# Last mixture of a decoder kernel: the gathers are spread over the pairs of experts, the answer rows are added on VectorE before they are turned, and unread matmuls stand in every second pair

## The reference, cut to what matters

```python
# x: [1792, 128] tokens, normalised; E = 32 experts, top 2, capacity 70 each
scores = softmax(router(x, stats(x)))            # [1792, 32]
w, e = top2(scores); w = w / w.sum(-1)
for each expert i:
    rows = the 70 best-scored tokens of those that chose i   # fewer: some slots stay empty
    h = silu(x[rows] @ gate_i.T) * (x[rows] @ up_i.T)        # 2 blocks of 128, and a
    y = h @ down_i.T + 0.05 * adapter_of_pair(x[rows])       # third from the pair's adapter
    out[rows] += w[rows, i] * y
x = x + out
```

## Time and profile before

| | us |
|---|---|
| median of 3 runs | 3799.75 (3795.43 to 3820.61) |
| profiled execution, its own time | 3812.16 |
| its span, first to last instruction | 3810.4 |
| last mixture: first gather issued | 3684.58 |
| first up matmul | 3689.53 |
| end of the last up (pair 15) | 3784.10 |
| first answer chunk read back | 3796.70 |
| last add to `x` | 3806.61 to 3807.23 |
| mean granted TensorE clock over the span | 0.948 |

### The profile page before, as it was taken

The page is one execution under the profiler, slowest core; times in us unless marked ns, Lnnn a source line. Parts: engine busy times, 40 slices in busy tenths (PEclk is TensorE's granted clock), DMA queues, the critical chain, the costliest instruction groups (busy, mean ns, idle before and its releaser), DMA issues. The chain is left out here.

```text
span 3810.4 us, 110666 instructions
## 1 busy us (share of the span) xinstructions
PE 3447.9 (90%) x46768; PEld 2411.7 (63%) x46768; DVE 2381.6 (63%) x4435; ACT 2087.9 (55%) x3581; POOL 1618.1 (42%) x1884
## 2 busy tenths in 40 slices
PE   7986669999999697889999999799999999999878
PEld 5654237777777344657777777343446777777548
DVE  5523568877776354468877776233667877777552
ACT  4333557777777222147777776334446777776511
POOL 1100157677674000047777664000336776776121
PEclk9999979999999798899999999899999999999967
DMA  4054136665664243036666564110015666656423
GB/s 164 2 227 168 47 84 155 153 159 144 154 156 97 51 117 82 4 88 152 149 160 148 149 158 100 47 61 23 13 43 140 156 154 152 159 145 153 123 68 106
DMA packets 206109, 439.22 MB, mean 115 GB/s; under 512 B 88210, under 2 KB 101111, under 8 KB 205448
## 3 DMA queue, kind: packets, MB, share of 16 engines
q1 hardware_dynamic: 202760, 430.07, 42.7%
q0 software_dynamic: 1440, 1.83, 0.2%
q10 hardware_dynamic: 1440, 0.52, 0.1%
HBM read 184.67 MB, written 5.40 MB: 50 GB/s over the span
## 5 line engine op out<-in xcount | busy, mean ns | idle before, releaser
L1562 DVE TENSOR_REDUCE x_bank_top<-ps 112x1 f32<-112x500 f32 x2304 | 1414.2, 672 | 447.8 <-PE ps L1264 440.8
L1410 ACT ACTIVATE x_probs_t<-ps 128x896 f32<-128x896 f32 x768 | 703.3, 916 | 127.6 <-PE ps L1285 122.6
L1264 PE MATMUL ps<-x_keys,x_queries 96*112 96x500 bf16 x2304 | 653.6, 382 | 42.5 <-DMA x_queries<-x_query_part 18.6
L1285 PEld LDWEIGHTS ps<-x_queries,x_keys 128*128 128x128 bf16 x9216 | 509.2, 97 | 245.6 <-issue 139.8
L1285 PE MATMUL ps<-x_queries,x_keys 128*128 128x112 bf16 x9216 | 580.9, 213 | 5.4 <-ACT x_probs_t L1410 4.2
L1299 PE MATMUL ps<-x_probs_t,x_values 128*32 128x112 f32 x18432 | 483.4, 261 | 8.9 <-ACT x_probs_t L1412 8.9
L1299 PEld LDWEIGHTS ps<-x_probs_t,x_values 128*32 128x32 f32 x18432 | 436.9, 110 | 70.1 <-issue 39.4
L1488 POOL TENSOR_TENSOR x_key_part<-x_key_whole,x_nothing 128x500 bf16<-128x500 f32 x270 | 337.3, 1249 | 256.8 <-ACT x_key_whole L1394 256.8
L1412 ACT ACTIVATE x_probs_t<-ps 128x448 f32<-128x448 f32 x768 | 414.5, 540 | 0.0
L1264 PEld LDWEIGHTS ps<-x_keys,x_queries 96*112 96x112 bf16 x2304 | 262.6, 131 | 170.9 <-DVE x_bank_top L1562 69.8
L1496 POOL TENSOR_TENSOR x_key_part<-x_key_left,x_nothing 128x500 bf16<-128x500 f32 x270 | 335.8, 1244 | 14.1
(11 more groups left out here) (510 smaller groups left out, 4332.1 us busy)
## 6 DMA issues: line engine op xcount, KB each, us to landing
x_keys<-x_key_part SPq DMA_DIRECT2D x1152, 192.0 KB, 3.8
x_ctx_t<-in_ctx_t SPq DMA_DIRECT2D x96, 750.0 KB, 6.2
cm_ctx_n<-in_ctx_n SPq DMA_DIRECT2D x32, 768.0 KB, 6.2
cm_ctx_t<-in_ctx_t SPq DMA_DIRECT2D x32, 750.0 KB, 8.6
x_queries<-x_query_part SPq DMA_DIRECT2D x558, 28.0 KB, 2.5
e_share<-m_weight_rows SPq DMA_DIRECT2D x32, 448.0 KB, 6.0
m_w<-in_L_ffn_experts SPq DMA_DIRECT2D x16, 768.0 KB, 5.7
e_share<-m_weight_rows SPq DMA_DIRECT2D x8, 896.0 KB, 5.3
```

Of the source, the lines that this page charges most:

```text
L1264: nc.tensor.matmul(ps[0:RW, n, 0:KB], queries[i // 2 % 2][0:TALL, p, i % 2, :], keys[i % 2][0:TALL, p, KB * n:KB * n + KB], start=True, st ...
L1285: mm = nc.tensor.matmul(ps[:, turned_bank(i, p) + c // VC, RW * (c % VC):RW * (c % VC) + RW], keys[i % 2][:, p, KT * c:KT * c + KT], queri ...
L1410: nc.scalar.activation(goal[:, 0:VR - 1], ps[:, bank:bank + VR - 1, 0:VC * RW], ACT.Exp, scale=scale).then_inc(exp_done, 1)
L1562: nc.vector.tensor_reduce(bank_top[0:RW, p, n:n + 1], ps[0:RW, n, 0:KB], AX_X, ALU.max).then_inc(topped, 1)
```

## The change

- The groups of tiles become 0 and 1, 2 and 3, 4 to 7, 8 to 11, 12 to 15, 16 and 17 (`GROUPS`).
- POOL issues only the first 8 gathers in a row. The other ten follow one at a time, gather 8 + n once up(n) is done, each ahead of the scatters of pair n - 1.
- PE runs six unread matmuls instead of four ahead of the first transposes, one more ahead of up(0), one behind it, and one ahead of up(n + 1) for n = 0, 2, ..., 14, into bank `TURN` and after a wait for the copy of the groups that pair n + 1 needs.
- ACT loads the table for Silu ahead of the first copy of a group, rather than at the first Silu.
- At the end PE waits for the last `weigh` and runs ten unread matmuls. DVE adds the two answer halves in SBUF (`join`), and PE turns the sum with one transpose for each block instead of two matmuls. DVE's order is join(0), join(1), add(0), join(2), add(1), join(3), add(2), add(3).

```diff
-    FIRST, GROUP = 2, 4
+    GROUP, AHEAD = 4, 8
+    GROUPS = (0, 2, 4, 8, 12, 16, TILES)
...
         last = (2 * CAP * (min(n, PAIRS - 1) + 1) - 1) // P
-        return max(last - FIRST, -1) // GROUP + 2
+        return next(g for g in range(len(GROUPS)) if GROUPS[g] > last)
...
-        return range(max(FIRST + GROUP * (g - 1), 0), min(FIRST + GROUP * g, TILES))
+        return range(GROUPS[g], GROUPS[g + 1])
...
-            def stay_busy(n):
+            def stay_busy(n, bank=RESULT + 1):
                 for _ in range(n):
-                    nc.tensor.matmul(ps[:, RESULT + 1, 0:CT], chip.mean[:], chunk[0], start=True, stop=True)
+                    nc.tensor.matmul(ps[:, bank, 0:CT], chip.mean[:], chunk[0], start=True, stop=True)
...
-            stay_busy(4)
+            stay_busy(6)
...
             for g in range(groups_for(0)):
                 turn_gathered(g)
+            stay_busy(1)
             up(0)
+            stay_busy(1)
             for g in range(groups_for(0), groups_for(1)):
                 turn_gathered(g)
             for n in range(PAIRS + 1):
                 if n + 1 < PAIRS:
+                    if n % 2 == 0:
+                        pe.wait_ge(s["gathered_kept"], groups_for(n + 1))
+                        stay_busy(1, TURN)
                     up(n + 1)
...
-            for c in range(CH):
-                pe.wait_ge(answers_landed[c], 16)
+            pe.wait_ge(s["weighted"], TILES)
+            stay_busy(10)
+            for c in range(CH):
+                pe.wait_ge(s["joined"], c + 1)
                 for t in range(TC):
-                    for k in range(2):
-                        mm = nc.tensor.matmul(ps[:, c, PAIR * t:PAIR * t + PAIR], back[c][:, t, k, :], chip.ident[0:PAIR, 0:PAIR], start=(k == 0), stop=(k == 1))
+                    mm = nc.tensor.transpose(ps[:, c, PAIR * t:PAIR * t + PAIR], back[c][:, t, 0, :], chip.ident[0:PAIR, 0:PAIR])
                 mm.then_inc(s["summed"], 1)
...
+            nc.scalar.preload_act_table_set("silu_and_others")
             for g in range(groups_for(0)):
                 keep_gathered(g)
...
-            for j in range(TILES):
+            def gather(j):
                 nc.gpsimd.indirect_dma_start(gathered[:, j, :], None, table, ...).then_inc(gathered_landed[j], 16)
-            pool.wait_ge(s["emptied"], 16 * CH)
-            for j in range(TILES):
+            def scatter(j):
                 r = slice(0, lines_in(j))
                 pool.wait_ge(s["weighted"], j + 1)
...
+            for j in range(AHEAD):
+                gather(j)
+            pool.wait_ge(s["emptied"], 16 * CH)
+            for n in range(PAIRS + 1):
+                if AHEAD + n < TILES:
+                    pool.wait_ge(s["up_done"], n + 1)
+                    gather(AHEAD + n)
+                for j in finished(n - 1):
+                    scatter(j)
...
-            for c in range(CH):
+            def join(c):
+                dve.wait_ge(answers_landed[c], 16)
+                nc.vector.tensor_tensor(back[c][:, :, 0, :], back[c][:, :, 0, :], back[c][:, :, 1, :], ALU.add).then_inc(s["joined"], 1)
+
+            def add(c):
                 goal = x[:, CB * c:CB * c + CB, 0:S]
                 dve.wait_ge(s["summed"], c + 1)
                 nc.vector.tensor_tensor(goal, goal, ps[:, c, 0:CT].rearrange("p (b s) -> p b s", s=S), ALU.add).then_inc(s["added"], 1)
+
+            join(0)
+            for c in range(1, CH):
+                join(c)
+                add(c - 1)
+            add(CH - 1)
```

More of the change, by code:

```diff
@@ L1970, in mixture_3 @@
             " gathered_turned gathered_kept up_done gate_kept hidden_ready down_done down_kept result_turned weighted slot_chain slots_ready"
-            " scattered summed added stored")
+            " scattered joined summed added stored")
     s = {k: chip.sem("m3_" + k) for k in sems.split()}
```

## The result

The changed kernel takes 3780.48 us in the median of 20 runs (3764.4 to 3792.89), the kernel before 3798.39 us over 20 (3782.85 to 3826.18). The ratio is 0.9941, with a 95% interval of 0.9925 to 0.9957. The forecast was 3778, range 3760 to 3798. The profiled execution takes 3780.02 us, 32.1 less than the one before, where the sum said 32.0. Of these 32.1 us the part that the change touches gives 30.6 (28.5 in the pairs, 2.1 at the end); 1.6 come from the stages ahead of it, which nobody changed: the first gather is issued at 3682.97 instead of 3684.58. The medians are only 17.9 us apart.

What follows compares the result with a forecast made beforehand. PE was taken as the bound, at half clock for much of the changed last 126 us. Terms -26.9 - 5.5 + 5.3 - 1.5 + 0.2 - 3.6 = -32.0 us from 3812.16 gave 3780; forecast 3778 us, range 3760 to 3798.

Steps and rivals of the forecast that it cites:

- The pairs: Everything up to the end of the last up: -28.4 us, ending at 3755.7 instead of 3784.1.
- The clock's term: From up(1) to the last up: full clock from the start takes 29.3 instead of 56.2 us, worth 26.9 us.
- Their price: Unread matmuls in pairs n = 2 to 14: seven of 0.75 us on PE's path, +5.3 us.
- the beginning: Around the first transposes and up(0): up(1) starts at about 3694.4 instead of 3695.98, -1.5 us.
- The stall: Issue gaps of PE in up(2) while the last gathers are issued: they go, -5.5 us.
- The end: Behind the last up: joins replace the sums in PSUM, add ends at 3803.6 instead of 3807.23, -3.6 us.
- The waits that I costed at nothing: In the pairs: waits for paced gathers, tile 15 the tightest with 2.0 us to spare, slot weights and weight loads add nothing.
- the clock rising one group earlier: Profiled execution 12.4 us above median: rise four pairs earlier (13.6 us) gives the old kernel 3798.5, the new still 3780.
- the prediction's own alternative: If the 12.4 us between profiled execution and median lie elsewhere, the new kernel takes 3767 us.
- Once there it stays: In the pairs: PE held 1.00 for 26.5 us with nothing unread among them, so full clock, once reached, stays.
- a single unread matmul in a pair raises it: In the pairs: should the clock fall, every second pair holds an unread matmul, denser at 448 columns for two weight loads.
- The rule of the Trainium skill that was weighed: PE's clock: by this rule busy pairs win full clock themselves; unread matmuls only cost time, as in a rival of chance 0.10.

Runs made afterwards that it cites:

- e2: Kernel before plus only the change's unread matmuls up to the last up, with its own groups, gathers and end: 3787.2 us, ratio 0.9957.
- e3: Changed kernel without any of its unread matmuls (four ahead of the first transposes, as before): 3794.1 us, ratio 0.9981.
- e7: Changed kernel without the eight unread matmuls in the pairs; those of the beginning and end stay: 3770.5 us, ratio 0.9911.
- e1: Kernel before, unedited, profiled once more: 3800.8 us in one run.
- e4: Changed kernel with all 18 gathers issued in a row again: 3780.8 us, ratio 0.993.
- e9: Kernel before with three more unread matmuls ahead of up(0) (six ahead of the first transposes, one before up(0)): 3805.9 us, ratio 0.9993.
- e12: Kernel before with two unread matmuls in a row ahead of up(3): 3780.9 us in one run.
- e10: Changed kernel with the unread matmuls of the beginning alone, none in the pairs or at the end: 3804.2 us, ratio 0.9993.
- e5: Kernel before with one single unread matmul added, ahead of up(3): 3791.9 us in one run.
- e6: Kernel before with one single unread matmul added, ahead of up(6): 3806.9 us in one run.
- e11: Changed kernel with four unread matmuls ahead of the first transposes and none around up(0): 3796.9 us, ratio 0.9989.

## Why the prediction was right, point by point

**The pairs** (-28.4 forecast, -28.5 measured in the profiles). The clock's term holds: 1.00 from the gathers to the last up. e2 shows that PE's unread matmuls alone bring it, and e3 that nothing else of the change does. Their price holds (0.76 us a pair; e7 gives 0.75), and so does the beginning: up(1) starts 9.96 us after the first gather was issued (at 3692.93 in the chain), against 11.40, -1.4 for -1.5.

**The stall** (-5.5) was wrong as a part of the change. It was in the profile before and gone after, so the sum came out, by luck: e1 hasn't got it, and e4 has the gathers in a row without it. Of eight profiles with the gathers in a row three show it (before, e9, e12), all three at half clock; of six with paced gathers none, though e10 has a late ACT. Whether pacing prevents it, at half clock, was not settled.

**The end** (-3.6 forecast) gave -2.1 in the first pair of profiles, and 2.6 by the means of all profiles but e10 (23.1 for the eight with the old end, 20.5 for five with the new): the direction held, with a last landing 1.1 us later (18.6 us behind the last up, where I took 17.5) and transposes 0.6 us slower than I took. The join took 0.69 us, as the row of its neighbour said. The ten unread matmuls show no gain; slowed by the half clock they ended at 3768.3, behind the first landing (its join starts at 3767.2) and not ahead of it as forecast, but well ahead of the last.

**The waits that I costed at nothing** cost nothing: tile 15's gather was issued at 3724.20, 3.7 us after the end of up(7) (3.6 forecast), and the longest of the 18 took 4.3 us to land (2.8 in the kernel before), median 2.6; in the pairs PE waited for nothing but one copy.

**The size against the median.** 12.4 us between the profiled execution and the median were put down to the clock rising one group earlier. e1, at about the median, refutes that: its clock rose at the same group. It lacks the stall, and its first gather is issued at 3677.2 instead of 3684.6, in stages that nobody changed; over all profiles that point lies between 3671 and 3692. If that reading goes, the prediction's own alternative is 3767, 13 us below what was measured. So the mechanism of the sum was right but for the stall, while the closeness of 3778 to the median of 3780.48 is in part luck. Against e1 the changed kernel's profile is 23.9 us shorter in the pairs, 2.7 at the end and 5.8 later at the first gather: 20.8 us, near the 17.9 between the medians.

**What I claimed beyond that** partly fell. "Once there it stays" is wrong: e9 and e10 lost the clock with PE idle for 2.3 and 2.7 us between up(0) and up(1). That a single unread matmul in a pair raises it is refuted by e5, e6 and the first of e11. What holds is a comparison of whole kernels. With unread matmuls at both places (around the first ups and in the pairs; changed, e2, e4) all 42 runs stay under 3794. With one of the two places, e9, e10 and e11 reach 3828 to 3841, while e7's seven runs end at 3775; with neither, e3 reaches 3817. The clock goes the same way: its mean over the whole span is 0.954 to 0.961 in the 42 runs and 0.956 to 0.959 in e7, but goes down to 0.942 in e10, 0.941 in e9, 0.944 in e3 and 0.947 in e11. e2 and e3 ran on one chip. e9, e10 and e11 ran on another, where no kernel with both places was run, so the chip isn't ruled out there: e2 differs from e9 only by the matmuls behind up(0) and in the pairs, and the times hardly overlap (3775 to 3794 against 3793 to 3841), but the intervals of their ratios do (0.9929 to 0.9985 against 0.9955 to 1.003). How those in the pairs do it wasn't seen: no profile caught the changed kernel with a fallen clock. e7, seven runs of 3768 to 3775, is the fastest median measured, but e10, the same up to the end of the pairs, had a median of 3804 on another chip. So it isn't shown that e7 beats the changed kernel reliably; a kernel that fills the wait ahead of up(1), rather than following it, was not tried.

The rule of the Trainium skill that was weighed ("TensorE: Matmul & The Clock Gate", Part 1, What's actually happening: activity releases the throttle) meets a stretch of e10 in which PE was busy for 105.6 of 105.6 us at 0.50. If activity means busy time, the traces disagree with it.

## What to carry to other kernels

Where PE is full of small matmuls and its clock is half, don't count on its being busy to bring the clock back. Look at what stood ahead of each fall and rise, and fill the waits before the small matmuls with wide unread ones, up to the last of these waits: filling only those ahead of up(0) gained nothing (e9). One profile isn't the kernel: take the same kernel's profile twice before a gap in it is counted as a gain. Judge such insurance by the spread over many runs and on more than one chip.

## What the runs showed of the hardware

PE lost the full clock after gaps with 2.3 us (e9) and 2.7 us (e10) of idle time between small matmuls, and then kept half clock through 105.6 us without a gap (e10), while in the same work it kept the full clock for 56 us (e7). Not every such gap did it: 2.58 us of idle ahead of 3671.50 in the changed kernel, between unread matmuls, left it at 1.00. One 128x448 matmul of two instructions among the small ones didn't raise it (e5, e6, e11). It rose behind two in a row (e12, one execution), as it did while a row of them ran ahead of the gathers, and behind a group of four transposes in some places (e3 at 3731, e5, e11) and not in others (e3 at 3702, e10). That the transposes themselves raised it wasn't tested. Three of fourteen profiles have a stretch of about 6 us in which single PE instructions start some 0.7 us apart or multiples of it (at 3704.54, 3706.70, 3708.12 and 3710.22 in the kernel before); its cause is open.
